# Retention: keys and attention's rows split in natural order and turned by transposing DMAs

## The reference

```
x = layernorm(x + attention(x))            # 16 heads, head gates, causal
x = layernorm(x + retention(x, context))   # the stage that is changed
x = layernorm(x + ffn(x))                  # fake-quantised, 1408 wide
```

```
q = xpos(x @ W_Q); k = xpos(context @ W_K, downscale); v = context @ W_V
sim = (q @ k.T) * decay_mask               # 16 heads of 32
ret = sim @ v; ret = (ret - mean) / sqrt(var + eps)
out = (ret * silu(x @ g_w.T + g_b)) @ out_w.T + out_b
```

## Time and profile before

| | |
|---|---|
| median of 3 runs | 1810.9 us (1810.56 to 1817.48) |
| the profiled execution | 1813.29 us, span 1811.4 us, mean PE clock 0.977 |
| busy in the span | PE 1671.2, DVE 1348.6, POOL 1065.7, ACT 1048.9 us |
| retention | from 964 to 1547 us |

### The profile page before, as it was taken

One profiled execution on the slowest core, in us unless ns is written; L12 is line 12 of the kernel. 1 busy time (PEld: TensorE's weight loads), 2 busy tenths in 40 slices (PEclk: granted clock), 3 DMA queues, 4 the chain that ended last, 5 costly groups with the idle time before them and its releaser, 6 DMA issues. The chain is left out here.

```text
span 1811.4 us, 36967 instructions
## 1 busy us (share of the span) xinstructions
PE 1671.2 (92%) x13294; PEld 755.4 (42%) x13294; DVE 1348.6 (74%) x3006; ACT 1048.9 (58%) x1857; POOL 1065.7 (59%) x1020
## 2 busy tenths in 40 slices
PE   5999999989999999998887989999999998799997
PEld 2433343334433344333233545555455544444433
DVE  6778657786677866677875678778778767788888
ACT  6476555665556655566653456465465454555577
POOL 4078777588675976859762665665675665000044
PEclk9999999999999999999898999999999999899999
DMA  8312102231012310222224243343333231651275
GB/s 287 118 28 72 39 22 59 75 96 39 24 51 80 105 31 24 63 88 60 93 94 168 66 111 112 100 130 95 93 119 93 72 99 48 242 209 47 70 267 204
DMA packets 141022, 176.33 MB, mean 97 GB/s; under 512 B 40360, under 2 KB 91048, under 8 KB 139944
## 3 DMA queue, kind: packets, MB, share of 16 engines
q1 hardware_dynamic: 135176, 165.24, 28.9%
q10 hardware_dynamic: 5664, 8.73, 1.6%
HBM read 106.12 MB, written 38.14 MB: 80 GB/s over the span
## 5 line engine op out<-in xcount | busy, mean ns | idle before, releaser
L1165 DVE CUSTOM_DVE_ANT_0 a_mx<-a_mx,a_mqk 128x128 f32<-128x128 f32 (+3 forms) x512 | 241.8, 511 | 139.8 <-PE a_mx L1365 136.4
L980 ACT ACTIVATE a_P<-a_mx 128x512 f32<-128x512 f32 (+3 forms) x417 | 186.6, 494 | 134.0 <-PE a_mx L1383 76.1
L1379 PE MATMUL a_mx<-a_Qs,a_Ks 128*128 128x512 f16 (+3 forms) x768 | 228.0, 332 | 18.4 <-ACT a_P L980 7.9
L1248 POOL TENSOR_TENSOR a_P<-a_P 128x512 f32<-128x512 f32 (+3 forms) x189 | 183.8, 1000 | 101.9 <-PE a_o L1395 77.6
L1365 PE MATMUL a_mx<-a_Ks,a_Qs 96*128 96x512 f16 (+3 forms) x768 | 222.9, 330 | 8.6 <-DVE a_nm L1165 2.1
L1248 POOL TENSOR_TENSOR a_P<-a_P,share 128x512 f32<-128x512 f32 (+3 forms) x199 | 184.5, 955 | 25.7 <-ACT share L980 18.4
L980 ACT ACTIVATE share<-a_mx 128x512 f32<-128x512 f32 (+3 forms) x303 | 135.6, 494 | 100.0 <-PE a_mx L1383 55.1
L1168 DVE TENSOR_REDUCE a_nm<-a_mx 128x1 f32<-128x512 f32 x256 | 164.7, 681 | 31.5 <-PE a_mx L1365 30.6
L2273 PE MATMUL r_pj<-share,cth 128*128 128x512 f16 x672 | 168.8, 387 | 3.0 <-PEq L123 2.3
L2273 PE MATMUL r_pj<-r_xTh,share 128*128 128x512 f16 x512 | 159.7, 385 | 7.6 <-DVE r_xTl L2119 7.5
L3017 PE MATMUL f_pj<-f_xqT,f_wgu 128*128 128x512 bf16 x704 | 156.7, 379 | 0.6 <-DVE f_xqT L2901 0.6
(11 more groups left out here) (306 smaller groups left out, 3987.7 us busy)
## 6 DMA issues: line engine op xcount, KB each, us to landing
x_scratch<-rows SPq DMA_DIRECT2D x60, 256.0 KB, 2.3
rows<-x_scratch SPq DMA_DIRECT2D x56, 256.0 KB, 4.0
lead<-in_xT SPq DMA_DIRECT2D x24, 512.0 KB, 4.6
lead<-in_ctxT SPq DMA_DIRECT2D x38, 256.0 KB, 3.2
h_scratch<-f_h SPq DMA_DIRECT2D x3, 2816.0 KB, 9.3
f_h<-h_scratch SPq DMA_DIRECT2D x3, 2816.0 KB, 10.8
a_Ks<-a_kph SPq DMA_DIRECT2D x256, 32.0 KB, 1.9
a_Qs<-a_qph SPq DMA_DIRECT2D x256, 32.0 KB, 1.9
```

Of the source, the lines that this page charges most:

```text
L980: act.activation(Pf[pf.at[key]][:, off:512], pb[:, off:512], ACT.Exp).then_inc(p_exp, 1)
L1165: dve.tensor_tensor_reduce(bank_of(it)[:, 0:n], bank_of(it)[:, 0:n], mqk[:, 512 - n:512], 1.0, -3e38, ALU.add, ALU.max, nm[:, col:col + 1] ...
L1248: pool.tensor_tensor(total[:, off:512], total[:, off:512], Pf[pf.at[key]][:, off:512], ALU.add).then_inc(add_pool, 1)
L1379: m = pe.matmul(pb[:, off:512], Ks[s][:, j, kt * P:(kt + 1) * P], Qs[s][:, j, qb * 512 + off:(qb + 1) * 512], start=True, stop=not diag)
```

## The change

Key tiles: after POOL's sum, ACT copies `m1` to f16 in natural order, POOL (not DVE) subtracts for the low part, and SP turns both halves, 128 x 1024, into `kT` with one transposing DMA. The wait for the last `R` goes with it from ACT to SP. x tiles but the first four: ACT and DVE split `xrow` in natural order into `x16`, SP turns it by one transposing DMA into one of two sets `xT`. K products have a stream of their own, half a unit earlier. x rows are fetched at 4h - 2.5 + 0.2k instead of 4h - 1.75 + 0.1k.

```diff
+            put("ACT", ("kt", b, t), 0.55, lambda: put("POOL", ("kt", b, t), 1.16, kt_split), lambda: n < 2 or has(("ktin", n - 2)))
...
+            put("SP", ("kt", b, t), 2.4, lambda: after(2.6, kt_in), lambda: half_done(b - 1, t // 4))
...
-        product(K0 if early else KV, [-2.1 + 0.2 * t] * 3 if early else [at_(0), at_(1), at_(2)], "K", ...)
+        product(K0 if early else KK, [-2.1 + 0.2 * t] * 3 if early else [at_(i) - 0.5 for i in range(3)], "K", ...)
...
-        pe_item(KV, at_(6), ("kt", b, t), 1.0, kt_made, ...)
...
+        def read():
+            put("ACT", ("xT", *key), 0.55, lambda: put("DVE", ("xT", *key), 0.84, split), lambda: n < 6 or has(("xT", *row(n - 2))))
+        def split():
+            xrow.give(key)
+            put("SP", ("xt", *key), 2.4, lambda: after(2.6, lambda: done.add(("xT", *key))),
+                lambda: n < 8 or has(("Gmm", *HALVES[n // 4 - 2], 3)))
...
+        turned = n < 4
...
-            rows(b, hf, i, 4 * h - 1.25 + 0.1 * i if h else -0.35 + 0.04 * i)
+            rows(b, hf, i, 4 * h - 2.5 + 0.2 * i if h else -0.35 + 0.04 * i)
...
+    kT = sb("kT", [P, 8, L], F16)
+    kTh, kTl = kT[:, 0:4, :], kT[:, 4:8, :]
+    kr = [sb(f"kr{i}", [P, 2, D], F16) for i in range(2)]
...
+    xT = [sb(f"xT{i}", [P, 8, 512], F16) for i in range(2)]
+    x16 = [sb(f"x16{i}", [P, 2, D], F16) for i in range(2)]
...   SP
+            elif kind == "kt":
+                w.wait_ge(kt_lo, n)
+                w.wait_ge(r_mm, retained(b - 1, t // 4))
+                sp.dma_start_transpose(kT[:, :, t * P:(t + 1) * P], kr[n % 2][:, :, :].rearrange("p s d -> p (s d)")
+                                       ).then_inc(kt_in[n % 2], 16)
+            elif kind == "xt":
+                w.wait_ge(x_lo, 4 * h + k + 1)
+                if h > 1:
+                    w.wait_ge(g_mm, num[("G", *HALVES[h - 2], 3)])
+                sp.dma_start_transpose(xT[h % 2][:, :, k * P:(k + 1) * P], x16[(k + 1) % 2][:, :, :].rearrange("p s d -> p (s d)")
+                                       ).then_inc(xt_in[k], 16)
...   ACT
+                w.wait_ge(k_pool, n)
+                if n > 2:
+                    w.wait_ge(kt_in[n % 2], 16 * ((n - 1) // 2))
+                act.activation(kr[n % 2][:, 0, :], m1[:, :], ACT.Copy).then_inc(kt_hi, 1)
...   DVE, K
-                    w.wait_ge(kt_mm, n - 1)
+                    w.wait_ge(kt_lo, n - 1)
...   POOL
+            elif kind == "kt":
+                w.wait_ge(kt_hi, n)
+                pool.tensor_tensor(kr[n % 2][:, 1, :], m1[:, :], kr[n % 2][:, 0, :], ALU.subtract).then_inc(kt_lo, 1)
...   PE
-            elif name == "kt":
-                w.wait_ge(k_pool, n)
-                for g in range(4):
-                    m = pe.transpose(pb[:, g * P:(g + 1) * P], m1[:, g * P:(g + 1) * P], identf[:, :])
...
-                w.wait_ge(kt_lo, num[("kt", b, 4 * hf + 3)])
+                for i2 in range(2):
+                    w.wait_ge(kt_in[i2], 16 * (4 * (2 * b + hf) + 4) // 2)
```

More of the change, by code:

```diff
@@ L1512, in k_made @@
             done.add(("Kmm", n))
-            put("DVE", ("K", b, t), 1.5, k_out, lambda: n < 1 or has(("ktmm", n - 1), ("kd", n - 1)))
+            put("DVE", ("K", b, t), 1.5, k_out, lambda: n < 1 or has(("ktlo", n - 1), ("kd", n - 1)))
         def k_out():
@@ L1520, in k_pool, with kt_split @@
             done.add(("kd", n))
[L1522 to L1527, removed]
+            put("ACT", ("kt", b, t), 0.55, lambda: put("POOL", ("kt", b, t), 1.16, kt_split), lambda: n < 2 or has(("ktin", n - 2)))
+        def kt_split():
+            done.add(("ktlo", n))
             if n == B * NT - 1:
@@ L1550, in kv_tile @@
         early = not b and t < 4
-        product(K0 if early else KV, [-2.1 + 0.2 * t] * 3 if early else [at_(0), at_(1), at_(2)], "K", (b, t), lambda: has(("split", b, t)), k_made)
+        product(K0 if early else KK, [-2.1 + 0.2 * t] * 3 if early else [at_(i) - 0.5 for i in range(3)], "K", (b, t), lambda: has(("split", b, t)), k_made)
         if b:
@@ L1565, in rows @@
         n = 4 * HALVES.index((b, hf)) + k
+        def read():
[4 more added lines that the diff above has]
+                lambda: n < 8 or has(("Gmm", *HALVES[n // 4 - 2], 3)))
         def made():
             xrow.give(key)
-            put("ACT", ("xT", *key), 0.55, lambda: put("DVE", ("xT", *key), 0.62, out),
-                lambda: n < 4 or has(("Gmm", *HALVES[n // 4 - 1], 3)))
+            put("ACT", ("xT", *key), 0.55, lambda: put("DVE", ("xT", *key), 0.62, out))
         def out():
@@ L1574, in out @@
             done.add(("xT", *key))
-        loads.append((place - 0.5 if n > 3 else -9.0, lambda: put("SP", ("xT", *key), 0.5, lambda: after(3.5, lambda: done.add(("xr", *key))),
-                                               lambda: len(xrow.busy) < 2, lambda: xrow.take(key))))
+        turned = n < 4
+        loads.append((-9.0 if turned else place, lambda: put(
+            "SP", ("xT", *key), 0.5, lambda: after(3.5, lambda: done.add(("xr", *key)) if turned else read()),
+            lambda: len(xrow.busy) < 2, lambda: xrow.take(key))))
+        if not turned:
+            return
         pe_item(X, place, ("xT", *key), 1.0, made, lambda: bank_ok("xT") and has(("xr", *key)), lambda: take(("xT", *key)))
@@ L1883, in state_of, with turned @@
         return s_dve, num[("S", b, ch - 1)]
+    def turned(n):
+        return xt_in[(n - 1) % 4], 16 * ((n - 1) // 4)
     def half_before(b, hf):
@@ L1988, in scalar @@
                 b, t = key
[L1989 to L1992, removed]
+                w.wait_ge(k_pool, n)
+                if n > 2:
+                    w.wait_ge(kt_in[n % 2], 16 * ((n - 1) // 2))
+                act.activation(kr[n % 2][:, 0, :], m1[:, :], ACT.Copy).then_inc(kt_hi, 1)
             elif kind == "xT":
                 b, hf, k = key
-                w.wait_ge(xt_mm, n)
                 if b or hf:
-                    w.wait_ge(g_mm, num[("G", *half_before(b, hf), 3)])
-                act.activation(xTh[:, :, k * P:(k + 1) * P], bank[pj.at[it]][:, :].rearrange("p (g s) -> p g s", g=4),
-                               ACT.Copy, scale=XS).then_inc(x_hi, 1)
+                    w.wait_ge(xr_in[k % 2], 16 * ((n + 1) // 2))
+                    if n > 6:
+                        w.wait_ge(*turned(n - 2))
+                    act.activation(x16[n % 2][:, 0, :], xrow[k % 2][:, :], ACT.Copy, scale=XS).then_inc(x_hi, 1)
+                else:
+                    w.wait_ge(xt_mm, n)
+                    act.activation(xT[0][:, 0:4, k * P:(k + 1) * P], bank[pj.at[it]][:, :].rearrange("p (g s) -> p g s", g=4),
+                                   ACT.Copy, scale=XS).then_inc(x_hi, 1)
             elif kind == "Q":
@@ L2281, in tensor @@
             work = (name, *key)
-            if part == 0 or name in ("kt", "S", "xT"):
+            if part == 0 or name in ("S", "xT"):
                 w.wait_ge(*after(work))
@@ L2318, in tensor @@
                 wn = "WQ" if name == "Q" else "gw"
-                w.wait_ge(x_lo, num[("xT", b, hf, 3)])
-                jobs = [(u[:, k, g * P:(g + 1) * P], v[:, k, :]) for u, v, k in mm3_jobs(Wh[wn], Wl[wn], xTh, xTl)]
+                h = 2 * b + hf
+                if h:
+                    for k in range(4):
+                        w.wait_ge(xt_in[k], 16 * h)
+                else:
+                    w.wait_ge(x_lo, 4)
+                jobs = [(u[:, k, g * P:(g + 1) * P], v[:, k, :])
+                        for u, v, k in mm3_jobs(Wh[wn], Wl[wn], xT[h % 2][:, 0:4, :], xT[h % 2][:, 4:8, :])]
                 product(pb[:, :], jobs, part, q_mm if name == "Q" else g_mm)
```

45 lines of the change are left out of this document (24 added, 21 removed).

## The result

| | median | runs |
|---|---|---|
| before | 1812.8 us | 1810.6 to 1817.5 |
| changed | 1784.6 us | 1783.0 to 1787.2 |

The ratio is 0.984, 95% interval 0.982 to 0.986: 28 us less, where 1783 and 30 us less were forecast. Beside the later experiments the same kernel gave 0.986 (0.984 to 0.989). The profiled execution took 1782.96 us, span 1781.1.

What follows compares the result with a forecast made beforehand. PE was taken to bound retention. Slots 27 plus waits 9, less 3 for POOL and 3 for SP, made 30 us off the profiled 1813.3, forecast 1783 us, range 1765 to 1811.

Steps and rivals of the forecast that it cites:

- The bound: PE bounds retention: busy 433.3 of 445 us in its middle, so what retention gains moves the end one to one.
- PE slots: Retention, PE: 60 turned tiles leave, 0.44 us each, 26.4 us; taken as 27, between 26 and 36.
- Waits that go: Retention, PE: waits for x's low part, banks and key tiles go, with slow clock 17 us; 9 kept, ends 0 and 17.
- the net 3: Retention: 9 us kept for removed waits, less 3 for POOL's delays and 3 for SP and the transfers.
- DVE: Retention: loses the key's low part, 21.6 us, x split from SBUF adds 7.6; 436 to 422 us, no cost.
- POOL: Retention: 32 added key subtractions, up to 39 us, hidden beneath PE; 3 us for delayed ql, ends 0 and 38.
- The first rival: Retention: POOL or a unit's chains take PE's place, key subtractions pushing ql out; 1800 to 1816 us, chance 0.15.
- K's chain: Retention: K's product to free m1 takes some 6 us, a K every 18; cost taken as 0, ends 0 and 3.6.
- SP and the transfers: Retention: 60 added transposing DMAs, issue 1.2 us, landing 3.5, hidden by the order's lead; 3 us taken.
- The slower rival: Half boundaries: transpositions stand behind long waits on SP, the first Q or A finds no tile; 1847 us, chance 0.11.
- The sum: Whole kernel: 27 + 9 - 3 - 3 = 30 us less, 1783 us; own range 1763 to 1798, chance 0.70.
- FFN: The stage behind retention uses nothing the change touches and keeps its length.

Runs made afterwards that it cites:

- idle_turns: The changed kernel with 240 transposes of the identity put back on PE ahead of K and Q products, waited for by nothing: 1804.4 us, ratio 0.995.
- two_sets: The kernel before with two sets of turned x and rows fetched earlier, everything still turned on PE: 1804.3 us, ratio 0.995.
- x_only: The changed kernel with keys turned on PE and split as before, K products at their old place; only x turned by DMA: 1798.6 us, ratio 0.993.
- k_place: The changed kernel with the K products back at their old place, half a unit later: 1800.6 us, ratio 0.993.
- k_only: The changed kernel with x turned on PE with one set as before; only keys turned by DMA, K still earlier: 1807.5 us, ratio 0.997.
- key_low_dve: The changed kernel with the key's low part subtracted on DVE instead of POOL: 1782.3 us, ratio 0.982.
- two_dmas: The changed kernel with each of the 60 new transposing DMAs cut in two of 128x512: 1796.2 us, ratio 0.991.

## Why the prediction was right

**The bound.** Right in the main. PE is still busy 431.1 of the middle's 445 us, against 433.3 before. Only two thirds of a slot's time reach the end, though (idle_turns); the prediction counted all.

**PE slots.** 27 us were forecast and 28.3 are gone from PE's stream. Their worth by idle_turns is 17 to 20. This is the term of the sum that was sized too high.

**Waits that go.** 17 us listed, 9 kept. The listed waits did go (7.5 to 1.1 for x's low part, 3.3 to 0 for the key), and the last half's first products of turned x run without a pause at full clock, as forecast: 16 matmuls in 3.63 us from 1440.15 on, granted 1.00. two_sets gives 9 us for the x part by itself, a part of which may be the lower clock behind the pauses. "Something else would have come a moment later" is what the masks show, 11.6 us where there were 0.8. The pause of 3.32 us at the fourth score group shows it in one place: the same group now has PE standing 1.34 us ahead of it and 2.85 us behind it. Standing as a whole rose by 2.9 us (0.7 in the second profile) instead of falling by the net 3.

**DVE.** Forecast 422 us, measured 428 in the stage, and "No cost: it is the second engine and gets lighter" was wrong as a judgement of single items. x's split reads SBUF and takes up to 1.75 us, 1.53 in the place shown here. DVE and PE in order of time in the changed kernel:

```profile
1045.00 1.14 DVE L2119 SCALAR_TENSOR_TENSOR cth<-lead,cth 128x512 f16<-128x512 f32 x1 [0.38 <-ACT cth L2019]
1046.06 1.53 DVE L2156 SCALAR_TENSOR_TENSOR r_x<-r_xrow,r_x 128x512 f16<-128x512 f32 x1
1047.51 2.47 DVE L2180 TENSOR_TENSOR r_AD<-r_pj,r_Dm 128x512 f32<-128x512 f32 x4
```

```profile
1048.25 4.45 PE L2316 MATMUL r_pj<-share,cth 128*128 128x512 f16 x12 [2.85 <-DVE r_AD L2180]
```

```profile
1049.00:1052.00 3.00, 3.00 (x9) 1.07 (x8) 2.86 (x6) 0.00 (x0) 1.40 (x2) 0.50 1.07 204
```

A context split and an x split, 2.5 us together, stand ahead of four masks; the banks of the score group stay full and PE stands 2.85 us, then runs at the lower of its clocks (1.2 GHz, granted 0.50 in the window above, columns as in the earlier trace rows): 12 matmuls take 4.45 us, against 12 x 0.216 = 2.6 at full clock. It is the longest pause in the middle of the stage. The x split is not by itself the reason for the masks' 11.6 us: x_only and k_place have the same split and wait 2.0 and 3.4 us for masks. What those two lack is the earlier K; k_only has it, without this split, and waits 4.3 us. Which part of the order makes the rest was not separated.

**POOL.** +38 forecast, +44 measured, the new subtraction itself 38.0 us as forecast (1.19 each) and the rest of POOL slower by some 6. Its effect on ql, kept at 3 us, is nil: 0.7 us of waits, where it was 3.4. Moving the subtraction to DVE brought 2 to 5 us (key_low_dve), with 4.5 us of waits for ql, so what it cost on POOL did not go by ql. The waits for `zl`, POOL's other subtraction, are new (4.0 and 2.8 us in the two profiles), but they stay without the keys' subtraction (3.8 us in key_low_dve). The first rival in its own form (ql pushed out) is refuted; what is left of it is that waits for the other engines fill a third of the slots' time.

**K's chain.** This is the step that failed. "K is also taken half a unit earlier (the KK stream). Nothing, except perhaps for the first score group of all". In truth half of the gain hangs on it: 13 to 16 us (k_place), as much as the keys' slots. The prediction looked at the time in which a key tile's buffer comes free, and gave K no other reader than the turned keys; the state's product S, which reads POOL's scaled copy, is where 5.7 us of the waits of k_place stand. Its sum had no term for the order, but took every freed slot as gained.

**SP and the transfers.** Issue 1.23 us and landing 3.2 to 3.5, forecast 1.2 and 3.5. SP's issuing made 233 us of the stage, where the forecast gave at most 249 to 321, and at this load PE waits 0.4 us for a turned tile. Whether SP costs more by what stands behind the transpositions is open: DVE waits 6.1 us for weight loads, 3.3 before. "About half the stage" as an argument for room did not hold: 60 issues more cost 9 us, mostly not by a turned tile. The slower rival named the halves' first Q or A as the place; two_dmas showed another place for the same kind of loss. The figure of the Trainium skill ("VectorE: DVE Perf Modes", the three transpose paths) of 1309 ns for a block by DMA, from which the prediction estimated 628 us for 480 blocks, does not add up that way here: eight blocks land together 3.2 us from issue.

**The sum.** 30 us were forecast and 28 measured, but part of that is luck. By the experiments the slots are worth 17 to 20 us and the x waits 9, which make the 28 without the 6 us taken off for POOL and SP. A slot term 7 to 10 us too high and costs of 6 us that do not show as such cancel each other, and the earlier K, without which the keys' slots bring nothing, was in the kernel but not in the sum. The lower end of the gain's own range is a slip too: 1813 - 53 is 1760, not 1763.

**FFN.** Its length is the same, as forecast: from the last matmul of retention to the end 274.7 us before, 273.8 after.

## What to carry to other kernels

Price a matmul by the distance of starts, and then take off what falls into time where PE would stand anyway: here a third, found with idle transposes that nobody waits for. A wait can move to the line of an added instruction; sum by what is waited for, not by line. When a change makes a producer's way longer, list all its readers; here a shift of half a step in the order was worth as much as the work removed. A queue that is half idle can still cost: follow what stands behind the added item, through every in-order list, to the bound engine.

## What the runs showed of the hardware

A transposing DMA's issue hardly grew with its size: 1.20 us for 128x512 and 1.23 us for 128x1024, both 16-bit, landing 2.4 and 3.2 to 3.5 us from issue. The longest of the 60 issues took 2.58 us, and plain DMA issues on SP also grew longer (the total of SP's issuing in the stage went from 137 to 233 us, 81 of it the new ones, so the old ones took 15 us more).

The lower clock of PE in the stage took 3.9 and 9.7 us in two profiles of the same kernel with nearly the same pauses. Behind the pause that ended at 1048.25 the granted clock was 0.50 until 1052 and 0.78 in the microsecond after it.
